# One core, four images: the low part of the normalised feature is subtracted on POOL instead of on the DVE

## The chip, the core and the metric

The kernel runs on one core of a Trainium2 chip. The metric is the device time in microseconds of one execution. The core's engines run side by side and meet at semaphores: TensorE (PE) multiplies, the DVE, ACT and POOL do elementwise work, and SP issues the DMAs.

## The reference

For each of four images (256 channels, 32 x 32 pixels) a block with a linear attention is followed by a block with a softmax attention over all 1024 pixels:

```
qkv  = x @ [wq, wk, wv]                       # 768 channels
dw   = depthwise 5x5 convolution of qkv       # 768 x 25 taps
pw   = grouped 1x1 convolution of dw
f    = concat(qkv, pw); relu(query), relu(key), value with a row of ones
out  = (value . key^T) . query, divided by its last row
x1   = batchnorm(proj . out) + x
norm = (x1 - mean(x1)) / sqrt(var(x1) + eps)   # over the pixels of a channel
F, G = f_w . norm + f_b, g_w . norm + g_b
A    = softmax(F^T . G)
y    = o_w . ((h_w . x1 + h_b) . A^T) + o_b + x1
```

## The kernel before

Each image is one `body(b)`; the first three run in a hardware loop, the last one stands behind it, without the work for a following image (`with_next` is false). While body b does the attention of image b, the engines also do most of the 5 x 5 convolution of image b + 1, in pieces that number tables place between the steps: DVE taps (`taps(n)`, L937), ACT products (`products(n)`, L748), and POOL adds (`conv_adds`, L1160), which add the ACT products to `conv`. ACT may be at most three products ahead of POOL, since `prod` has three buffers. POOL has 54 such adds for each body in the loop, numbered from 0, and none of the next image's in the last body.

Every engine runs its instructions in the order in which they are written. There is no scheduler; the order around the change is set by hand, for POOL with `RSTD_AT = (19, 20)`: after 19 and after 20 adds it takes the two small power instructions `rstd` (L1154) that give 1/sqrt(var + eps) of channel halves c = 0 and 1.

Around the change a body goes as follows. The DVE gets `x1`, its statistics (L1035 to L1041), and, after each `rstd`, `normalise(c)` (L1045), which writes the normalised half c into `nf` (a view of `rows`). ACT rounds it to the matmul type, `hi` (L848). The DVE subtracts: `lo = nf - hi` (L1066), two instructions of 128 x 1024, one for each half. PE computes F and G in eight units of 512 columns (`split_product`, the loop over `D_FG`): in each four matmuls that need only `hi` (L447, L448) and two that need `lo` (L451). Only in the first unit PE waits for `norm_lo`, between the fourth and the fifth matmul, and it wants both halves. ACT then writes `f_hi` or `g_hi` of the unit (L852), and the DVE `f_lo` or `g_lo` (L1072), which frees one of two PSUM banks for the unit after the next. The DVE has no tap between L1066 and the second `f_lo`, as its table is `TAPS_FG = (0, 0, 1, 1, 2, 1, 1, 1)`. The softmax attention (`energy`, L544, and so on) follows when all eight units are done.

There is a second subtraction of the same size, `split_lo` (L347), for the low part of the next image's input; in the loop it runs on POOL at a body's start, in the first image on the DVE.

Of the kernel before, what the change touches and what calls it, by code (L numbers as in the profile page):

```python
# [25 lines left out]
ALU = mybir.AluOpType  # L26
ACT = mybir.ActivationFunctionType
AX = mybir.AxisListType
F32 = mybir.dt.float32
# [3 lines left out]
B = 4  # L33
# [3 lines left out]
CK = C // P  # L37
# [76 lines left out]
POOL_ADDS = len(ADD_SEQ)  # L114
# [25 lines left out]
ROWS_ACT = (0, 0, 0, 0, 1, 0, 0, 0)  # L140

RSTD_AT = (19, 20)

FIRST_TAPS = 62

# [19 lines left out]
def conv_seq_kernel(nc, x, wqkv, dw, pw, proj, bn, fgw, hw, ow, l1b, masks, out):  # L165
    with ExitStack() as ctx:
        def sb(name, shape, dt=F32):
            return ctx.enter_context(nc.sbuf_tensor(name, shape, dt))

        def sem(name):  # L170
            return ctx.enter_context(nc.semaphore(name))


        hi = sb("hi", [P, CK, N], F32R)
        lo = sb("lo", [P, CK, N], F32R)
# [35 lines left out]
        nf = x_in = qp  # L211
# [51 lines left out]
        norm_ready = sem("norm_ready")  # L263
        norm_hi = sem("norm_hi")
        norm_lo = sem("norm_lo")
# [35 lines left out]
        def product_count(b, n):  # L301
            return len(FIRST_POOL_SEQ) + (PRODUCTS + LATE) * b - PRODUCTS + n

        def add_count(b, n):
            return len(FIRST_ADD_SEQ) + (POOL_ADDS + LATE - 1) * b - POOL_ADDS + n

        def late_product_count(b, n):
            return product_count(b, PRODUCTS) + n

        def late_add_count(b, n):  # L310
            return add_count(b, POOL_ADDS) + n
# [30 lines left out]
        def split_lo(engine, b):  # L342

            for h in range(2):
                engine.wait_ge(hi_ready, 2 * b + h + 1)
                cols = slice(h * HALF, (h + 1) * HALF)
                engine.tensor_tensor(lo[:, :, cols], x_in[:, :, cols], hi[:, :, cols].bitcast(F32),  # L347
                                     ALU.subtract).then_inc(lo_ready, 1)
# [23 lines left out]
        def inner(image, i):  # L372

            dy, dx = shift(i)
            return image[:, max(0, -dy):SIDE - max(0, dy), max(0, -dx):SIDE - max(0, dx)]

        def square(image):
            return image.rearrange("p (y x) -> p y x", x=SIDE)
# [12 lines left out]
        @block.sync  # L391
        def _(sp):
            def load_x(b):
                sp.dma_start(x_in[:], x[b]).then_inc(x_loaded, 16)

            def load_residual(b):
                sp.dma_start(x1[:], x[b]).then_inc(res_loaded, 16)

            def body(b, with_next, with_second):
                for q in range(2):  # L400
                    cols = slice(q * HALF, (q + 1) * HALF)
                    sp.wait_ge(pv_free, pv_count(b, 2 * (q + 1)))
                    sp.dma_start(out[b][:, :, cols], x1[:, :, cols]).then_inc(stored, 16)
                    if q == 0 and with_second:

                        sp.wait_ge(t_full, 16 * (b + 1))
                        load_x(b + 2)

                sp.wait_ge(stored, 32 * (b + 1))
                if with_next:  # L410
                    load_residual(b + 1)

            sp.dma_start(wqkv_st, wqkv).then_inc(qkv_loaded, 16)
            load_x(0)
            sp.dma_start(mask_sb[:], masks).then_inc(conv_loaded, 16)
            sp.dma_start(dw_sb[:], dw).then_inc(conv_loaded, 16)
            sp.dma_start(bn_sb[:], bn).then_inc(conv_loaded, 16)
            sp.dma_start(l1b_sb[:], l1b).then_inc(w_loaded, 16)
            sp.dma_start(fg_st, fgw).then_inc(w_loaded, 16)
            sp.dma_start(hw_st, hw).then_inc(w_loaded, 16)  # L420
            sp.dma_start(ow_st, ow).then_inc(w_loaded, 16)
            sp.dma_start(pw_sb[:], pw).then_inc(w_loaded, 16)
            sp.dma_start(proj_sb[:], proj).then_inc(w_loaded, 16)

            sp.wait_ge(d_full, D_FIRST)
            load_x(1)

            sp.wait_ge(a_free, A_FIRST)
            load_residual(0)
            with sp.Fori(0, B - 2) as b:  # L430
                body(b, True, True)
            body(B - 2, True, False)
            body(B - 1, False, False)
# [494 lines left out]
        def _(dve):  # L928
# [74 lines left out]
            def body(b, with_next):  # L1003
# [39 lines left out]
                def normalise(c):  # L1043
                    dve.wait_ge(rstd_ready, CK * b + c + 1)
                    dve.tensor_scalar(nf[:, c, :], x1[:, c, :], mv[:, c, 0:1], stat_rstd[:, c:c + 1],  # L1045
                                      ALU.subtract, ALU.mult).then_inc(norm_ready, 1)

                for u in range(D_PROJ):
                    c, h = u // 2, u % 2
# [10 lines left out]
                normalise(0)  # L1060
                taps(TAPS_NORM[1])
                normalise(1)
                for c in range(CK):
                    dve.wait_ge(norm_hi, CK * b + c + 1)
                    dve.wait_ge(norm_ready, CK * b + c + 1)
                    dve.tensor_tensor(lo[:, c, :], nf[:, c, :], hi[:, c, :].bitcast(F32),  # L1066
                                      ALU.subtract).then_inc(norm_lo, 1)
                for u in range(D_FG):
                    w, c, h = u // 4, (u // 2) % 2, u % 2
                    cols = slice(h * HALF, (h + 1) * HALF)  # L1070
# [74 lines left out]
            with dve.Fori(0, B - 1) as b:  # L1145
                body(b, True)
            body(B - 1, False)


        @block.gpsimd  # L1150
        def _(pool):
            def rstd(b, c):
                pool.wait_ge(var_ready, CK * b + c + 1)
                pool.tensor_tensor(stat_rstd[:, c:c + 1], stat_ve[:, c:c + 1], minus_half[:, c:c + 1],  # L1154
                                   ALU.pow).then_inc(rstd_ready, 1)

            def add(total, m, i):

                total, product = inner(square(total), i), inner(square(prod[:, m % PROD_BUFS, :]), i)
                pool.tensor_tensor(total, total, product, ALU.add).then_inc(conv_pool, 1)  # L1160

            def conv_adds(b, first, last):

                batch_0 = isinstance(b, int) and b == 0
                seq, adds = (FIRST_POOL_SEQ, FIRST_ADD_SEQ) if batch_0 else (POOL_SEQ, ADD_SEQ)
                for m in range(first, min(last, len(adds))):
                    t, i = adds[m]
                    n = seq.index((t, i)) + 1
                    pool.wait_ge(prod_ready, n if batch_0 else product_count(b, n))

                    if (t, i - 1) in adds:
                        before = adds.index((t, i - 1)) + 1
                        pool.wait_ge(conv_pool, before if batch_0 else add_count(b, before))
                    add(conv[:, t, :], m, i)

            def late_adds(b):

                for m in range(LATE - 1):
                    pool.wait_ge(prod_ready, late_product_count(b, m + 2))
                    if m > 0:  # L1180
                        pool.wait_ge(conv_pool, late_add_count(b, m))
                    add(late, m, LATE_SEQ[m + 1][1])

            pool.memset(raw[:], 0.0).then_inc(images_cleared, 1)

            pool.wait_ge(constants_set, 1)
            pool.wait_ge(bn_ve_ready, 1)
            pool.tensor_tensor(bn_tmp, bn_ve, minus_half, ALU.pow).then_inc(bn_rstd_ready, 1)
            conv_adds(0, 0, POOL_ADDS)
            with pool.Fori(0, B - 1) as b:  # L1190
                split_lo(pool, b + 1)
                late_adds(b)
                conv_adds(b + 1, 0, RSTD_AT[0])
                rstd(b, 0)
                conv_adds(b + 1, RSTD_AT[0], RSTD_AT[1])
                rstd(b, 1)
                conv_adds(b + 1, RSTD_AT[1], POOL_ADDS)
            late_adds(B - 1)
            rstd(B - 1, 0)
            rstd(B - 1, 1)  # L1200


def _partitioned(a, rows):
# [48 lines left out]
```

## Time and profile before

| what | value |
|---|---|
| median of 3 runs | 824.53 us (824.3 to 825.83) |
| span of the profiled execution | 823.0 us |
| PE busy | 687.7 us, 84% |
| DVE busy | 655.2 us, 80% |
| POOL busy | 544.9 us, 66% |
| ACT busy | 477.8 us, 58% |
| mean granted TensorE clock | 0.944 of full |

The span runs from the first to the last instruction of the profiled execution. That execution has no time of its own among the three runs; the median of these is 1.53 us above its span, which is what lies around the span. Busy shares are means over stages with different limits, so the stage around the subtraction is read by itself below. A granted clock of 1.00 is TensorE's 2.4 GHz, 0.50 its 1.2 GHz.

### The profile page before, as it was taken

The numbers are of one execution on the slowest core, as the hardware profiler recorded it, in microseconds if no ns is written. First come the engines' busy times: TensorE is split into PE (matmuls) and PEld (weight loads), VectorE is DVE, ScalarE is ACT, GpSimd is POOL, SyncE is SP. The second block draws the span as 40 slices with busy tenths as digits, with TensorE's granted clock in tenths as the row PEclk, the third lists the DMA queues.
The fourth block names the chain that finished last, engine by engine and source line by source line (L and its number), as shares of the span: only waits on it lengthen the run. The fifth ranks groups of instructions, "written<-read, shape, count | busy, mean of one in ns | idle before, by whom it ended". The sixth has DMA issues, their size and how long they took to land.

```text
span 823.0 us, 9427 instructions
## 1 busy us (share of the span) xinstructions
PE 687.7 (84%) x2892; PEld 466.7 (57%) x2892; DVE 655.2 (80%) x797; ACT 477.8 (58%) x703; POOL 544.9 (66%) x248
## 2 busy tenths in 40 slices
PE   4999888779678899789677899789677994788997
PEld 4744577566456467576456457475456454455843
DVE  6999599899779889989779889989779899334520
ACT  4944458674568668673568668773567646213520
POOL 3498958896779798895769889785769858100000
PEclk9999999899799999889799999889799998999999
DMA  5000020000000130000000021000000001000000
GB/s 196 2 0 1 0 103 1 2 0 1 0 2 1 38 115 2 0 0 0 0 0 0 26 84 44 0 0 0 0 0 0 26 26 51 1 0 1 1 25 25
DMA packets 4801, 15.93 MB, mean 19 GB/s; under 512 B 672, under 2 KB 928, under 8 KB 3744
## 3 DMA queue, kind: packets, MB, share of 16 engines
q1 hardware_dynamic: 4768, 15.56, 5.1%
q8 instruction: 12, 0.20, 0.1%
q14 instruction: 21, 0.17, 0.1%
HBM read 11.37 MB, written 4.19 MB: 19 GB/s over the span
## 4 chain that ended last, share of the span: by engine, by line
PE 49%; DVE 32%; issue 12%; ACT 4%; DMA 1%; DVEq 0%; ACTq 0%; SPq 0%
DVE ps L937 17%; PE ps L568 13%; PE ps L544 7%; PE ps L494 7%; PE ps L517 3%; PE ps L622 3%; PE ps L451 3%; PE ps L447 3%; PE ps L448 3%; DVE sd L981 2%; PE ps L559 2%; DVE kv L999 2%; DVE den L997 2%; DVE small L1090 2%; PE ps L504 1%
## 5 line engine op out<-in xcount | busy, mean ns | idle before, releaser
L1160 POOL TENSOR_TENSOR conv<-conv,prod 128x930 f32<-128x930 f32 (+4 forms) x192 | 435.8, 2301 | 101.4 <-ACT prod L748 97.9
L937 DVE SCALAR_TENSOR_TENSOR ps<-raw,dw_sb,ps 128x960 f32<-128x960 f32 (+4 forms) x290 | 348.5, 1202 | 12.8 <-issue 4.8
L748 ACT ACTIVATE prod<-raw,dw_sb 128x930 f32<-128x930 f32 (+4 forms) x228 | 248.7, 1115 | 74.9 <-POOL conv L1160 62.1
L568 PE MATMUL ps<-kv,oc 128*128 128x512 f32 x256 | 111.6, 594 | 2.8 <-ACT kv L878 2.8
L1160 POOL TENSOR_TENSOR rows<-rows,prod 128x930 f32<-128x930 f32 (+4 forms) x36 | 83.2, 2312 | 15.0 <-ACT prod L748 12.3
L517 PE MATMUL ps<-sd,rows 128*128 128x144 f32 x256 | 56.0, 372 | 32.5 <-DVE kv L999 19.3
L568 PEld LDWEIGHTS ps<-kv,oc 128*128 128x128 f32 x256 | 48.3, 190 | 61.4 <-issue 57.4
L517 PEld LDWEIGHTS ps<-sd,rows 128*128 128x128 f32 x256 | 45.8, 246 | 45.3 <-DVE kv L999 28.0
L1090 DVE TENSOR_REDUCE small<-ps 128x1 f32<-128x1024 f32 x32 | 39.1, 1221 | 28.9 <-PE ps L544 28.9
L862 ACT ACTIVATE rows<-ps,small 128x1024 f32<-128x1024 f32 x32 | 35.7, 1116 | 45.3 <-DVE small L1090 45.3
L622 PE MATMUL ps<-oc,proj_sb 128*128 128x512 f32 x128 | 56.0, 595 | 2.1 <-DVE kv L999 1.3
L559 PE MATMUL ps<-mask_sb,rows 128*128 128x128 f32 x256 | 36.5, 282 | 24.7 <-ACT kv L878 14.7
L878 ACT COPY kv<-ps 128x512 f32<-128x512 f32 x64 | 34.6, 587 | 26.5 <-PE ps L559 26.5
L544 PE MATMUL ps<-g_hi,f_hi 128*128 128x512 f32 x128 | 43.1, 419 | 7.5 <-DVE g_lo L1072 7.5
L559 PEld LDWEIGHTS ps<-mask_sb,rows 128*128 128x128 f32 x256 | 27.4, 140 | 38.3 <-ACT kv L878 24.1
L447 PE MATMUL ps<-hi,wqkv_hi 128*128 128x512 f32 x96 | 39.4, 410 | 10.3 <-DVE lo L347 10.3
L774 ACT COPY oc<-ps 128x512 f32<-128x512 f32 x32 | 16.4, 599 | 53.1 <-PE ps L528 53.1
L447 PE MATMUL ps<-hi,fg_hi 128*128 128x512 f32 x64 | 31.8, 496 | 17.9 <-ACT hi L848 11.8
L766 ACT ACTIVATE kv<-ps 128x256 f32<-128x256 f32 x68 | 30.5, 449 | 23.9 <-PE ps L583 21.5
L1154 POOL TENSOR_TENSOR small<-small 128x1 f32<-128x1 f32 x8 | 4.9, 612 | 59.3 <-DVE small L1041 59.3
L622 PEld LDWEIGHTS ps<-oc,proj_sb 128*128 128x128 f32 x128 | 24.0, 190 | 31.7 <-issue 28.7
L544 PE MATMUL ps<-g_lo,f_hi 128*128 128x512 f32 x128 | 41.1, 403 | 0.0
(97 smaller groups left out, 1172.3 us busy)
## 6 DMA issues: line engine op xcount, KB each, us to landing
rows<-x_dram SPq DMA_DIRECT2D x4, 1024.0 KB, 4.8
x<-x_dram SPq DMA_DIRECT2D x4, 1024.0 KB, 4.9
out_dram<-x SPq DMA_DIRECT2D x8, 512.0 KB, 3.1
conv<-wqkv_dram SPq DMA_DIRECT2D x1, 768.0 KB, 4.6
conv<-fg_dram SPq DMA_DIRECT2D x1, 512.0 KB, 5.4
proj_sb<-proj_dram SPq DMA_DIRECT2D x1, 512.0 KB, 7.3
pw_sb<-pw_dram SPq DMA_DIRECT2D x1, 384.0 KB, 6.5
conv<-hw_dram SPq DMA_DIRECT2D x1, 256.0 KB, 5.6
```

The costliest lines, as they stand in the source:

```text
L447: pe.matmul(dst, lh, rh, start=(k == 0), stop=False)
L494: mm = pe.matmul(dst, diagonal(t, i), view, start=(i == 0), stop=(i == taps - 1))
L517: mm = pe.matmul(dst[:, h * SDW:(h + 1) * SDW], qp[:, h, j * P:(j + 1) * P], sd[:, h, :], start=True, stop=True)
L544: mm = pe.matmul(ps[:, pair + h, :], lhs, g[:, k, h * HALF:(h + 1) * HALF], start=(s == 0), stop=(s == len(steps) - 1))
L559: mm = pe.transpose(ps[:, 4 + u, j * P:(j + 1) * P], rows[:, i % ROW_BUFS, key:key + P], ident)
L568: mm = pe.matmul(ps[:, 4 + c, :], ht[:, j, c * P:(c + 1) * P], pt[:, j, :], start=(j == 0), stop=(j == NB - 1))
L622: mm = pe.matmul(d_bank(s), proj_sb[:, k, c * P:(c + 1) * P], oc[:, k, h * HALF:(h + 1) * HALF], start=(k == 0), stop=(k == 2 * CK - 1))
L748: act.activation(dst, view, ACT.Copy, scale=weight(t, i)).then_inc(prod_ready, 1)
L862: act.activation(rows[:, i % ROW_BUFS, :], ps[:, pair:pair + 2, :].rearrange("p a n -> p (a n)"), ACT.Exp, bias=neg_max[:, i:i + 1], accum ...
L937: return dve.scalar_tensor_tensor(dst, view, w, before, ALU.mult, ALU.add)
L1090: dve.tensor_reduce(neg_max[:, i:i + 1], ps[:, pair:pair + 2, :].rearrange("p a n -> p (a n)"), AX.X, ALU.max, negate=True).then_inc(max_r ...
L1160: pool.tensor_tensor(total, total, product, ALU.add).then_inc(conv_pool, 1)
```

## The change

The DVE no longer issues the two subtractions of a body. POOL issues them: in a loop body after add 22 and ahead of add 23 of the next image's convolution, in the last body right behind the second `rstd`. The operands, the waits (`norm_ready`, `norm_hi`) and the semaphore that is raised (`norm_lo`) are the same.

```diff
 RSTD_AT = (19, 20)
+NORM_LO_AT = 23
...
                 taps(TAPS_NORM[1])
                 normalise(1)
-                for c in range(CK):
-                    dve.wait_ge(norm_hi, CK * b + c + 1)
-                    dve.wait_ge(norm_ready, CK * b + c + 1)
-                    dve.tensor_tensor(lo[:, c, :], nf[:, c, :], hi[:, c, :].bitcast(F32),
-                                      ALU.subtract).then_inc(norm_lo, 1)
...
+            def norm_split(b):
+                for c in range(CK):
+                    pool.wait_ge(norm_ready, CK * b + c + 1)
+                    pool.wait_ge(norm_hi, CK * b + c + 1)
+                    pool.tensor_tensor(lo[:, c, :], nf[:, c, :], hi[:, c, :].bitcast(F32),
+                                       ALU.subtract).then_inc(norm_lo, 1)
...
                 rstd(b, 1)
-                conv_adds(b + 1, RSTD_AT[1], POOL_ADDS)
+                conv_adds(b + 1, RSTD_AT[1], NORM_LO_AT)
+                norm_split(b)
+                conv_adds(b + 1, NORM_LO_AT, POOL_ADDS)
             late_adds(B - 1)
             rstd(B - 1, 0)
             rstd(B - 1, 1)
+            norm_split(B - 1)
```

POOL's queue in the loop body, before, from the second `rstd` on (`small` is the result of `rstd`; the adds write `conv`):

```order
L1154 TENSOR_TENSOR small<-small 128x1 [waits var_ready]
L1169 REGISTER_ALU
L1173 REGISTER_ALU [waits prod_ready]
L1160 TENSOR_TENSOR conv<-conv,prod 128x32x30 [waits conv_pool]
L1169 REGISTER_ALU
L1173 REGISTER_ALU [waits prod_ready]
L1160 TENSOR_TENSOR conv<-conv,prod 128x32x30 [waits conv_pool]
L1173 REGISTER_ALU [waits prod_ready]
```

The same place of the changed kernel, from the second of these adds (21) to add 23:

```order
L1163 TENSOR_TENSOR conv<-conv,prod 128x32x30 [waits conv_pool]
L1176 REGISTER_ALU [waits prod_ready]
L1163 TENSOR_TENSOR conv<-conv,prod 128x32x31 [waits conv_pool]
L1157 TENSOR_TENSOR lo<-rows,hi 128x1024 [waits norm_hi,norm_ready] x2
L1172 REGISTER_ALU
L1176 REGISTER_ALU [waits prod_ready]
L1163 TENSOR_TENSOR conv<-conv,prod 128x32x31 [waits conv_pool]
```

The two subtractions stand between adds 22 and 23, which follow one another before; in the changed file the adds have line 1163 and the subtractions line 1157.

The DVE's queue in the loop body, before, around its subtractions:

```order
L937 SCALAR_TENSOR_TENSOR ps<-raw,dw_sb,ps 128x960 [waits conv_dve]
L1044 REGISTER_ALU
L1045 TENSOR_SCALAR rows<-x,mv,small 128x1024 [waits rstd_ready]
L1066 TENSOR_TENSOR lo<-rows,hi 128x1024 [waits norm_ready,norm_hi] x2
L1071 ISA
L1072 SCALAR_TENSOR_TENSOR f_lo<-ps,l1b_sb,f_hi 128x512 [waits fg_hi_ready]
L1071 REGISTER_ALU
```

And in the changed kernel:

```order
L938 SCALAR_TENSOR_TENSOR ps<-raw,dw_sb,ps 128x960 [waits conv_dve]
L1045 REGISTER_ALU
L1046 TENSOR_SCALAR rows<-x,mv,small 128x1024 [waits rstd_ready]
L1067 ISA
L1068 SCALAR_TENSOR_TENSOR f_lo<-ps,l1b_sb,f_hi 128x512 [waits fg_hi_ready]
```

Behind the second `normalise` the DVE now has only the wait for the first `f_hi`. No tap moved into the place.

## Rows read from the trace of the kernel before

**Rows 1.** The page: the chain that ended last, shares of the span by engine.

```profile
PE 49%; DVE 32%; issue 12%; ACT 4%; DMA 1%; DVEq 0%; ACTq 0%; SPq 0%
```

**Rows 2.** The longest waits of PE: us in total, times, longest.

```profile
PE ps L451 <- DVE lo L1066: 10.8, 4, 3.7
```

**Rows 3.** Timeline of body 1, DVE: start, us, instructions, idle before.

```profile
390.44 1.17 DVE L1045 TENSOR_SCALAR rows<-x,mv,small 128x1024 f32<-128x1024 f32 x1
...
392.66 1.60 DVE L1045 TENSOR_SCALAR rows<-x,mv,small 128x1024 f32<-128x1024 f32 x1
394.19 6.57 DVE L1066 TENSOR_TENSOR lo<-rows,hi 128x1024 fp32r<-128x1024 f32 x2
402.80 0.75 DVE L1072 SCALAR_TENSOR_TENSOR f_lo<-ps,l1b_sb,f_hi 128x512 fp32r<-128x512 f32 x1 [2.04 <-ACT f_hi L852]
```

**Rows 4.** Timeline of body 1, POOL, in narrow windows: adds 20 to 24 singly.

```profile
388.80 2.27 POOL L1160 TENSOR_TENSOR conv<-conv,prod 128x960 f32<-128x960 f32 x1
...
391.02 2.70 POOL L1160 TENSOR_TENSOR conv<-conv,prod 128x960 f32<-128x960 f32 x1
...
393.68 2.76 POOL L1160 TENSOR_TENSOR conv<-conv,prod 128x992 f32<-128x992 f32 x1
...
396.40 3.27 POOL L1160 TENSOR_TENSOR conv<-conv,prod 128x992 f32<-128x992 f32 x1
...
403.94 2.28 POOL L1160 TENSOR_TENSOR conv<-conv,prod 128x960 f32<-128x960 f32 x1 [4.27 <-ACT prod L748]
```

**Rows 5.** Timeline of body 1, ACT and PE around the wait.

```profile
394.30 1.06 ACT L848 ACTIVATE hi<-rows 128x1024 fp32r<-128x1024 f32 x1 [0.16 <-DVE rows L1045]
...
400.81 1.22 PE L451 MATMUL ps<-lo,fg_hi 128*128 128x512 f32 x2 [3.59 <-DVE lo L1066]
...
402.07 0.69 ACT L852 ACTIVATE f_hi<-ps,l1b_sb 128x512 fp32r<-128x512 f32 x1 [6.71 <-PE ps L451]
402.66 1.13 ACT L748 ACTIVATE prod<-raw,dw_sb 128x960 f32<-128x960 f32 x1
404.63 0.69 ACT L852 ACTIVATE f_hi<-ps,l1b_sb 128x512 fp32r<-128x512 f32 x1 [0.85 <-PE ps L451]
```

**Rows 6.** Body 0: add 22 on POOL, the DVE's pair.

```profile
206.32 2.75 POOL L1160 TENSOR_TENSOR conv<-conv,prod 128x992 f32<-128x992 f32 x1
...
206.82 6.56 DVE L1066 TENSOR_TENSOR lo<-rows,hi 128x1024 fp32r<-128x1024 f32 x2
```

**Rows 7.** The other subtraction of this size, by source line and timeline.

```profile
L347 POOL TENSOR_TENSOR lo<-rows,hi x6: 2361/2366/2382, 114.7 to 488.0; 128x1024 fp32r<-128x1024 f32 x6
L347 DVE TENSOR_TENSOR lo<-rows,hi x2: 1219/1222/1226, 9.0 to 10.1; 128x1024 fp32r<-128x1024 f32 x2
...
298.20 4.69 POOL L347 TENSOR_TENSOR lo<-rows,hi 128x1024 fp32r<-128x1024 f32 x2
```

**Rows 8.** Timeline of the last body: DVE, ACT, PE.

```profile
735.11 0.81 DVE L1045 TENSOR_SCALAR rows<-x,mv,small 128x1024 f32<-128x1024 f32 x1 [0.44 <-POOL small L1154]
741.04 2.36 DVE L1066 TENSOR_TENSOR lo<-rows,hi 128x1024 fp32r<-128x1024 f32 x2 [5.11 <-ACT hi L848]
...
743.45 0.73 PE L451 MATMUL ps<-lo,fg_hi 128*128 128x512 f32 x2 [0.25 <-DVE lo L1066]
...
748.56 0.69 ACT L852 ACTIVATE f_hi<-ps,l1b_sb 128x512 fp32r<-128x512 f32 x1 [1.09 <-PE ps L451]
...
751.80 0.69 ACT L852 ACTIVATE g_hi<-ps,l1b_sb 128x512 fp32r<-128x512 f32 x1 [1.10 <-PE ps L451]
```

**Rows 9.** Windows: stretch, length, busy (x) of PE, PEld, DVE, ACT, POOL, PEclk.

```profile
396.00:406.20 10.20, 6.61 (x16) 4.63 (x16) 6.26 (x4) 3.28 (x4) 5.93 (x3) 0.50 0.00 0
...
744.05:747.45 3.40, 3.40 (x10) 2.62 (x9) 0.75 (x1) 1.36 (x2) 0.00 (x0) 0.50 0.00 0
747.50:757.00 9.50, 8.68 (x35) 5.75 (x33) 4.50 (x6) 3.98 (x6) 0.00 (x0) 1.00 0.00 0
```

## The prediction

> **What bounds the kernel now.** I read the chain that ended last first: PE and DVE hold it together (49% and 32%), ACT has 4%, and POOL does not appear [rows 1]. So POOL's 66% busy share is beside the path, and work given to POOL is free as long as nobody on the path waits for it. The waits of PE then show whether the subtraction is on the path: PE waits for `lo` four times, once in each body, 10.8 us together [rows 2]. It is work that PE waits for directly, not cover work. The question is therefore not how much DVE time is freed, but when the second half of `lo` is there.
>
> In body 1 the DVE takes up the pair at 394.19 and ends it at 400.76, 3.3 us for each instruction [rows 3], where the same operation on a DVE beside an idle POOL takes 1.22 [rows 7], and 1.2 in the last body, where POOL has no adds either (2.36 for both) [rows 8]. The rows of POOL say what is in between [rows 4]. Add 22 ends at 396.44, and the first subtraction, 1.2 us long, then ends near 397.5. Add 23, begun at 396.40 by its record, lasts 3.27 in place of some 2.2 and ends at 399.67; the second subtraction ends 1.1 us later. The two engines take turns: a subtraction is held until the running add ends, and the next add is held until the subtraction ends. The pair is thus a sum of waits: add 22's rest (2.2 us), 1.2, add 23 (2.2), 1.2.
>
> The rule for this is in the Trainium skill, "SBUF — State Buffer", section "Who interferes with whom": DVE and GpSimd share one port pair as an exclusive lock, for a whole instruction. The trace agrees (3.3 us against 1.22). It alone would speak for the change, since a pair on one engine has no such turn to wait for.
>
> **The change, part by part.**
>
> *The DVE loses two instructions a body.* That frees 6.57 us of each of three bodies and 2.36 us of the last. All of it becomes waiting: the next thing in the DVE's order is the first `f_lo`, which waits for ACT's `f_hi`, which waits for PE, which waits for `lo`; no tap stands between (the order in the section on the change). Gain from the DVE's time: 0. What hides that nothing is gained is a wait of 2.04 us [rows 3] that becomes about 8.9 (2.04 + 6.57 and the delay below).
>
> *POOL's price.* It runs the same subtraction in 2.37 us, and two in a row in 4.69 [rows 7]. The shape there is 2 x 512 columns, here 1024 in one piece; adds of 960 columns take 2.27 and 2.28 when undisturbed [rows 4], which for 1024 would be 2.4. Bounds for the pair: below 4.5 (twice the undisturbed 960-column add, less a little for overlap), above 5.5 (twice the 2.76 of a disturbed add). I take 4.69, the row of the same operation, since the DVE is idle meanwhile.
>
> *When POOL begins, three loop bodies.* POOL takes the pair behind add 22. Adds 20 and 21 and the two `normalise` run as before, so add 22 ends at 396.44 again. By then both halves of `hi` are ready (the second ends at 394.30 + 1.06 = 395.36 [rows 5]), so nothing else is waited for. Add 22 begins next to the end of `normalise` (394.26), and 394.26 + 2.2 gives 396.4: its stretch comes from there, not from the subtraction behind it. The pair ends at 396.40 + 4.69 = 401.09, against 400.76: +0.33 us. Body 0: 206.32 + 2.75 = 209.07, less the same 0.04 of overlap, plus 4.69 is 213.72, against 206.82 + 6.56 = 213.38: +0.34 [rows 6]. Body 2 repeats body 1. Three bodies: +1.0 us (bounds +0.4 with 4.5, +3.4 with 5.5).
>
> *Add 23 and what is queued behind it.* It now begins at 401.1 instead of 396.4 and, no longer held, ends at about 403.4 instead of 399.67. Nobody waits for it in that time: POOL stood idle for 4.27 us until the product of add 24 came [rows 4]. That product begins at 402.66 and takes 1.13 [rows 5]; it comes 0.33 later, so add 24 begins near 404.3 with 0.9 us to spare. Cost: 0. If the cover were gone, each microsecond that POOL is late would push the products that come before `g_hi` in ACT's order, and through them PE, one for one.
>
> *The last body.* Here POOL is idle, so there is no turn to save. The DVE begins at 741.04 and ends the pair at 743.40, and PE resumes at 743.45 [rows 8]. POOL can begin at 741.05, when the first half of `hi` is there, and ends at 741.05 + 4.69 = 745.74. PE: +2.34 us (bounds +2.1 and +3.1).
>
> On that ratio the Trainium skill, "GPSIMD Engine Reference", section "Elementwise — side-by-side cycle accounting", gives 4497 against 2293 ns for an add of 2048 float32 columns; half of it, an estimate, is 2.25 us for one subtraction, and by it the sum below would be about 1 us smaller. The rows show 2.37 against 1.22, and I go by them.
>
> *TensorE's clock.* In body 1 the granted clock is 0.50, the 1.2 GHz level, from 396.0 to 406.2 [rows 9]: it falls after PE had stood idle for the first `hi`, and stays low through the idle 3.59 us before L451; it rises 5.4 us after PE resumes at 400.81. While it is low a unit takes 404.63 - 402.07 = 2.56 us [rows 5]; at 2.4 GHz two take 751.80 - 748.56 = 3.24, so 1.62 each [rows 8]. A microsecond of work at the low level thus costs 0.37. In the loop bodies PE's idle time hardly changes (3.59 to 3.9 us), and I leave the clock as it is. In the last body PE was idle for only 0.25 us before L451, and the clock was low for 3.4 us, 744.05 to 747.45. After the change it is idle there for about 2.6 us, more like a loop body. If the clock rises when it does now, 1.65 us of low work remain and 0.65 us comes back; if it rises 5.4 us after PE resumes, 2.0 us more low work costs +0.74. I take +0.4, nearer to the second, since the idle time is nearer to that of the loop bodies.
>
> **Sum.** 1.0 + 2.34 + 0.4 = +3.7 us. On the profiled execution's span that is 823.0 + 3.7 = 826.7; the median stands 1.53 above that span, so the time is 828.2 us, 0.45% more than before. With the bounds: +0.4 + 2.1 - 0.65 = +1.9, and +3.4 + 3.1 + 0.74 = +7.2 (831.7), which needs every instruction disturbed by an engine that is idle. A change within 0.2% (1.65 us) is about what a measurement of this kernel cannot tell from none.
>
> **The rivals.**
>
> *Shorter adds.* If the DVE's held subtraction also slows the add that runs, add 22 falls from 2.76 to 2.2 and the pair ends 0.55 - 0.33 = 0.2 us earlier than before. For: both records are long. Against: `normalise` explains it to a tenth. Three times -0.2, and 2.34 with nothing for the clock, is +1.7: 826.2. Chance 0.07.
>
> *Faster, by the clock.* The low level in a loop body costs 5.4 x 0.37 = 2.0 us. If another rhythm around the wait (POOL's pair ends 0.3 us later, the engines' loads differ) let the clock rise as soon as PE resumes, three bodies would give back 6.0, and the sum is 1.0 + 2.34 - 6.0 = -2.7: 821.8. For: in the last body the low stretch is only 3.4 us. Against: the clock falls at 396.0, before anything differs. It decides when less than about 2.5 us of low work remain in each loop body. Chance 0.04.
>
> *POOL becomes late.* If the pair takes 5.5 or more, or adds run longer than the 0.9 us to spare, add 24 slips and ACT's products with it: +3.4 from the pair and 2.34 + 0.4, some +6: 830.7. For: POOL's records stretch to 3.27. Against: they do so only beside a DVE that works. Chance 0.07.
>
> *It doesn't matter.* Later waits in the loop bodies (PE for the attention's rows) swallow the 1.0 us, and the last body's clock returns 0.65 and some of what is queued behind is hidden: +1.2, 825.7. Against: the chain runs through PE, `f_lo` and `energy` without a gap. Chance 0.06.
>
> The forecast has the rest, 0.76. Its own range is 826.4 to 829.9. The time is named for it alone; the range 826.0 to 830.2 leaves out the clock rival, most of the last one and about half of the late POOL, with a small part of the forecast, under 2 in 10. Faster by over 0.2%: 0.04. Within 0.2%: the last rival, part of the first, and a thin edge of the forecast, 0.11. Slower: 0.85.
>
> **What the profile of the changed kernel would show.** Right: in body 1 two POOL subtractions of 2.35 each directly behind add 22, the DVE idle for about 8.9 us before its first `f_lo`, PE's wait for `lo` at 3.9 us in loop bodies and 2.6 in the last (some 14 us in all, from 10.8), add 23 of 2.3 us and a short idle time before add 24. Wrong: subtractions over 2.6 us, POOL idle before them (then `hi` is late, not the adds), an add 22 of 2.2 us, or ACT waiting for POOL before `g_hi`. A low stretch of the clock in the last body much over 3.4 us puts me at the upper end; low stretches under 8 us in loop bodies put me at the lower.

## The result and the profile after

| | before | changed |
|---|---|---|
| median | 824.3 us (822.79 to 828.62, 15 runs) | 829.55 us (827.88 to 831.78, 15 runs) |
| span of the profiled execution | 823.0 us | 827.4 us |
| mean granted clock | 0.944 | 0.94 |

The ratio is 1.006, with a 95% interval of 1.0046 to 1.0075. By the medians the changed kernel is 5.2 us slower where 3.7 were forecast, and its median lies inside the stated range of 826.0 to 830.2 us, near the upper end.

First the waits of PE, which answer to [rows 2]: us in total, times, longest.

```profile
PE ps L452 <- POOL lo L1157: 13.9, 4, 3.9
```

PE waits for `lo` as often as before, now for POOL, and 3.1 us longer in all (10.8 before).

The timeline of body 1 follows, first POOL and then the DVE, ACT and PE. This execution stood 1.39 us later than the one of before already when the body's first `rstd` began (385.86 against 384.47), so times are compared from that instruction on.

```profile
385.86 0.55 POOL L1150 TENSOR_TENSOR small<-small 128x1 f32<-128x1 f32 x1 [8.74 <-DVE small L1042]
...
390.19 7.63 POOL L1163 TENSOR_TENSOR conv<-conv,prod 128x960 f32<-128x960 f32 x3
397.78 4.65 POOL L1157 TENSOR_TENSOR lo<-rows,hi 128x1024 fp32r<-128x1024 f32 x2
402.39 2.31 POOL L1163 TENSOR_TENSOR conv<-conv,prod 128x992 f32<-128x992 f32 x1
405.60 2.27 POOL L1163 TENSOR_TENSOR conv<-conv,prod 128x960 f32<-128x960 f32 x1 [0.90 <-ACT prod L749]
...
404.46 0.75 DVE L1068 SCALAR_TENSOR_TENSOR f_lo<-ps,l1b_sb,f_hi 128x512 fp32r<-128x512 f32 x1 [8.81 <-ACT f_hi L853]
...
403.74 0.69 ACT L853 ACTIVATE f_hi<-ps,l1b_sb 128x512 fp32r<-128x512 f32 x1 [7.00 <-PE ps L452]
...
408.29 0.69 ACT L853 ACTIVATE f_hi<-ps,l1b_sb 128x512 fp32r<-128x512 f32 x1 [0.30 <-PE ps L452]
...
402.49 1.22 PE L452 MATMUL ps<-lo,fg_hi 128*128 128x512 f32 x2 [3.80 <-POOL lo L1157]
```

The pair stands right behind adds 20 to 22 and takes 4.65 us. It ends at 402.43, that is 16.57 after the `rstd` (402.43 - 385.86); the DVE's pair of before ended at 400.76, 16.29 after it [rows 3]. Add 23 is back at 2.31 us, from 3.27 [rows 4], and POOL still idles for 0.90 before add 24. The DVE waits 8.81 us for the first `f_hi`. The first `f_hi` begins 17.88 after the `rstd` (17.60 before), the third 22.43. The third of before, and the last `g_hi` of its last body, for the comparison further down:

```profile
406.79 0.69 ACT L852 ACTIVATE f_hi<-ps,l1b_sb 128x512 fp32r<-128x512 f32 x1 [0.45 <-PE ps L451]
...
756.47 0.69 ACT L852 ACTIVATE g_hi<-ps,l1b_sb 128x512 fp32r<-128x512 f32 x1 [0.75 <-PE ps L451]
```

The last body, again POOL, ACT and PE:

```profile
731.91 0.55 POOL L1150 TENSOR_TENSOR small<-small 128x1 f32<-128x1 f32 x1 [28.38 <-DVE small L1042]
...
742.59 4.65 POOL L1157 TENSOR_TENSOR lo<-rows,hi 128x1024 fp32r<-128x1024 f32 x2 [6.07 <-ACT hi L849]
...
760.95 0.69 ACT L853 ACTIVATE g_hi<-ps,l1b_sb 128x512 fp32r<-128x512 f32 x1 [0.72 <-PE ps L452]
...
747.30 1.22 PE L452 MATMUL ps<-lo,fg_hi 128*128 128x512 f32 x2 [2.65 <-POOL lo L1157]
```

And windows of both places: stretch, length, busy time (and instructions) of PE, PEld, DVE, ACT and POOL, and the granted clock.

```profile
397.20:407.40 10.20, 6.40 (x16) 4.50 (x15) 1.13 (x2) 2.80 (x4) 9.30 (x5) 0.50 0.00 0
...
745.40:752.20 6.80, 4.90 (x12) 3.84 (x13) 1.11 (x2) 1.37 (x2) 1.84 (x1) 0.50 0.00 0
```

In the loop body the stretch at the half clock is as long as before, 10.2 us [rows 9]. In the last body it is 6.8 us, from 3.4.

Where did the 4.4 us between the two spans come from? The first `rstd` of the first body and that of the last body, before and then after:

```profile
197.11 0.55 POOL L1154 TENSOR_TENSOR small<-small 128x1 f32<-128x1 f32 x1 [7.00 <-DVE small L1041]
...
730.47 0.55 POOL L1154 TENSOR_TENSOR small<-small 128x1 f32<-128x1 f32 x1 [28.49 <-DVE small L1041]
```

```profile
198.36 0.55 POOL L1150 TENSOR_TENSOR small<-small 128x1 f32<-128x1 f32 x1 [7.01 <-DVE small L1042]
...
731.91 0.55 POOL L1150 TENSOR_TENSOR small<-small 128x1 f32<-128x1 f32 x1 [28.38 <-DVE small L1042]
```

1.25 us lie ahead of the first of them, where nothing was changed. The clock can account for them: ahead of that `rstd` it is low for 10.2 us in the profile of before and for 13.7 in the one after, and 3.4 us more at the prediction's 0.37 are 1.26. The three loop bodies add (731.91 - 198.36) - (730.47 - 197.11) = 0.19 us, and what follows the last one adds (827.4 - 731.91) - (823.0 - 730.47) = 2.96 us.

### The profile page after: what moved, and what is told of

Same layout as the page of the kernel before. It is cut to its first block, busy times and chain, and to the rows that moved or that the text cites. A ratio compares the mean times of both kernels' runs of the same rounds, so it can differ in the third digit from the quotient of the medians.

```text
span 827.4 us, 9427 instructions
## 1 busy us (share of the span) xinstructions
PE 689.5 (83%) x2892; PEld 468.4 (57%) x2892; DVE 634.0 (77%) x789; ACT 477.4 (58%) x703; POOL 560.1 (68%) x256
## 4 chain that ended last, share of the span: by engine, by line
PE 50%; DVE 29%; issue 11%; ACT 5%; POOL 2%; DMA 1%; POOLq 0%; DVEq 0%; ACTq 0%; SPq 0%
DVE ps L938 16%; PE ps L569 13%; PE ps L545 7%; PE ps L495 7%; PE ps L518 4%; PE ps L452 3%; PE ps L448 3%; PE ps L623 3%; PE ps L449 3%; DVE sd L982 2%; PE ps L560 2%; PE ps L505 2%; POOL lo L1157 2%; DVE kv L1000 2%; DVE small L1086 2%
## 5 line engine op out<-in xcount | busy, mean ns | idle before, releaser
L1068 DVE SCALAR_TENSOR_TENSOR f_lo<-ps,l1b_sb,f_hi 128x512 fp32r<-128x512 f32 x16 | 12.0, 750 | 51.1 <-ACT f_hi L853 51.1
```

## The experiments

Each time below is a median and stands against the median of the kernel before on the same chip. The difference in us that follows a ratio is worked out from the ratio; that of the two medians can be some 2 us away from it. "Low" is a stretch at the half clock, and a "last stretch" runs from the first `rstd` of the last body to the end.

**The change in one part of the program at a time.** The first kernel leaves the last body's pair on the DVE:

```diff
                 normalise(1)
+                for c in range(CK) if not with_next else ():
+                    dve.wait_ge(norm_hi, CK * b + c + 1)
+                    dve.wait_ge(norm_ready, CK * b + c + 1)
+                    dve.tensor_tensor(lo[:, c, :], nf[:, c, :], hi[:, c, :].bitcast(F32),
+                                      ALU.subtract).then_inc(norm_lo, 1)
...
-            norm_split(B - 1)
```

> POOL subtracts in the three loop bodies, the DVE in the last one. Theory (what counts is when the second half of lo is there): POOL's pair ends 0.3 us later than the DVE's in each loop body, and part of that is given back by the clock, so +0.2 to +1.0 us against the kernel before, and PE's wait for lo in the loop bodies near 3.9 us, in the last 0.25. Rival (the loop bodies carry what the medians show beyond my sum, +5.25 measured against about 3 in the last body): +2.3 us or more.

The second leaves the loop bodies' pair on the DVE (`if with_next`, and `norm_split(b)` taken out of the loop).

> The DVE subtracts in the loop bodies, POOL in the last. Theory: nearly all of the loss is here, 2.34 us from the slower pair and some 0.4 to 0.7 from the clock, +2.5 to +3.1 us against the kernel before. Rival (the loss is spread over the four bodies): +1.3 us, a quarter of +5.25.

Measured: the loop alone 827.09 against 825.1 us, ratio 1.0016 (1.0002 to 1.0031), +1.3 us. The last body alone 828.68 against 825.1, ratio 1.0041 (1.0024 to 1.0057), +3.4 us. Together 4.7, most of it in the last body, as the theory has it. +3.4 is a little above the 2.5 to 3.1 expected, which its interval holds. An even split is out, by the last stretches of the profiles above all. In the profile of the first, PE waits 11.1 us for POOL three times and 0.3 for the DVE; its last stretch takes 826.1 - 733.49 = 92.6 us, as before (92.5), the second 827.3 - 731.68 = 95.6, as the changed kernel (95.5). +1.3 is above my 0.2 to 1.0; whether it is different from nothing the control at the end puts in doubt.

**One add earlier, one add later.**

```diff
-NORM_LO_AT = 23
+NORM_LO_AT = 22
```

> As the changed kernel, with the pair one add earlier, behind add 21. Theory: POOL begins when the first half of hi is there (394.2 in the times of the kernel before) and ends at 398.8 instead of 401.1, 2.3 us earlier in each loop body, and with the last body's loss of 3 the sum is -1.9 x 3 + 3 = -2.7 us against the kernel before. Rival (another thing than the pair sets the end of the stage, such as POOL being late for add 24 and ACT's products behind it): within 1 us of the changed kernel, so about +4 to +5.

> As the changed kernel, with the pair one add later, behind add 23. Theory: one add of 2.3 us more ahead of PE's wait in each loop body, +6.9 us against the changed kernel, about +11 to +12 against the kernel before, and PE waits 6.2 us for lo in a loop body. Rival (the wait has slack behind it): under +3 us against the changed kernel.

Measured: one earlier 820.37 against 825.1, ratio 0.9936 (0.9914 to 0.9958), -5.3 us; one later 838.08 against 825.1, ratio 1.0132 (1.0099 to 1.0165), +10.9 us. The direction is the theory's in both. The later place costs about what was expected (+11 to +12; the medians are 13.0 apart). The earlier place gives twice what was expected, and more than the shift of the pair itself explains: the pair ends 2.1 us earlier in each loop body, and from the first body's `rstd` to the last body's it takes 523.0 us (723.05 - 200.03) against 533.55, 3.5 us less for each. Its timeline in body 1, POOL and PE:

```profile
387.93 4.91 POOL L1163 TENSOR_TENSOR conv<-conv,prod 128x960 f32<-128x960 f32 x2
393.41 4.66 POOL L1157 TENSOR_TENSOR lo<-rows,hi 128x1024 fp32r<-128x1024 f32 x2 [0.57 <-DVE rows L1046]
398.02 4.60 POOL L1163 TENSOR_TENSOR conv<-conv,prod 128x992 f32<-128x992 f32 x2
...
398.12 1.22 PE L452 MATMUL ps<-lo,fg_hi 128*128 128x512 f32 x2 [1.97 <-POOL lo L1157]
```

And the window of its low stretch:

```profile
395.20:402.10 6.90, 4.93 (x12) 3.37 (x11) 0.75 (x1) 1.87 (x3) 6.90 (x4) 0.51 0.00 0
```

PE's wait in body 1 falls from 3.80 to 1.97 us, and the low stretch falls from 10.2 to 6.9. In the later place it is 13.7 us long, with a wait of 5.8 to 6.1. Its windows, of body 1 and of the last body:

```profile
400.90:414.50 13.60, 6.92 (x15) 4.96 (x16) 1.06 (x2) 3.51 (x5) 10.42 (x5) 0.50 0.00 0
752.50:762.60 10.10, 8.21 (x18) 5.95 (x19) 1.50 (x2) 1.43 (x3) 3.91 (x2) 0.50 0.00 0
```

In the loop bodies the low stretch moves with PE's wait; in the expectation for the earlier place I had left it as it was. In the last body it doesn't: nothing differs there from the changed kernel, PE waits for 1.79 us, less than the 2.65 of that kernel, and the low stretch is 10.2 us in place of 6.8. It begins earlier there, so the four matmuls ahead of the wait are slow too, and that shortens the wait.

The same place without the last body's loss (pair behind add 21 in the loop, the DVE's pair in the last body):

> POOL subtracts behind add 21 in the loop bodies, the DVE in the last. Theory: the loop's gain of the run with the pair behind add 21, without the last body's loss of about 3 us: -8 to -9 us against the kernel before (that run was at -5.3). Rival (the last body's loss depends on where the clock stands, not on the pair): -5 to -6.

Measured: 816.43 against 823.85, ratio 0.9911 (0.9886 to 0.9935), -7.3 us. It lies between the -8 to -9 of the theory and the -5 to -6 of the rival, and 2 us below the run with POOL in the last body, with intervals that overlap, so the times don't decide between the two. The profile does: it gives the last stretch as 92.6 us (813.2 - 720.58) against 95.5 (818.6 - 723.05). The last body's 3 us are there again.

**The engines' turns.** The kernel before, with POOL held out of the pair's way:

```diff
                 rstd(b, 1)
-                conv_adds(b + 1, RSTD_AT[1], POOL_ADDS)
+                conv_adds(b + 1, RSTD_AT[1], 22)
+                pool.wait_ge(norm_lo, CK * b + CK)
+                conv_adds(b + 1, 22, POOL_ADDS)
```

> The kernel before, with one wait added on POOL: in a loop body it takes add 22 only when both of the DVE's subtractions are done. Theory (the DVE's pair is long only because it takes turns with POOL's adds): each subtraction takes 1.2 us, the pair ends at 396.6 instead of 400.76 in each loop body, -4.1 us three times, and the clock stays low for a shorter stretch: -12 to -16 us against the kernel before, PE's wait for lo near 0.2 in all four bodies. Rival (POOL, held for 3 us and with adds 22 and 23 still to do, becomes late for ACT's products and gives the gain back later in the stage): under -6 us. Rival (a DVE subtraction is slow beside other engines' traffic anyway): it stays at 3.3 us and the time rises.

Measured: 810.5 against 823.85 us, ratio 0.9827 (0.9812 to 0.9841), -14.3 us, inside the expected -12 to -16. It is the fastest kernel of this study, faster than every version of the change. The DVE's subtractions in its profile by source line (min/median/max in ns, first and last start):

```profile
L1066 DVE TENSOR_TENSOR lo<-rows,hi x8: 1210/1221/1226, 209.0 to 731.2; 128x1024 fp32r<-128x1024 f32 x8
```

Its timeline in body 1: the pair, POOL behind it, and PE.

```profile
391.07 2.43 DVE L1066 TENSOR_TENSOR lo<-rows,hi 128x1024 fp32r<-128x1024 f32 x2
...
393.66 20.12 POOL L1160 TENSOR_TENSOR conv<-conv,prod 128x992 f32<-128x992 f32 x9 [3.06 <-DVE lo L1066]
...
394.24 1.05 PE L451 MATMUL ps<-lo,fg_hi 128*128 128x512 f32 x2
```

All eight subtractions take 1.2 us, where the six of the loop bodies took 3.3, with nothing changed but POOL's absence: that POOL's adds stretch the pair is shown. That the two engines take whole turns, and don't merely slow each other, is read from the rows of before, whose ends such turns give to a tenth; no run separates the two. PE goes from the fourth matmul to the fifth without a wait. The low stretch of body 1 is still 6.8 us long:

```profile
391.50:398.20 6.70, 5.83 (x14) 4.58 (x15) 2.75 (x3) 2.76 (x4) 4.54 (x2) 0.50 0.00 0
```

POOL idles for 3.06 us and then works through nine adds without a gap; that backlog costs little here. The Trainium skill, "SBUF — State Buffer", section "Who interferes with whom", calls the port pair that the DVE and GpSimd share an exclusive lock, which a DVE instruction with two SBUF inputs and a GpSimd instruction that reads SBUF contend for. The trace agrees: 1.2 us alone, 3.3 beside the adds.

With the hold one add earlier (21 in place of 22):

> As the run that holds POOL ahead of add 22, with the hold one add earlier. Theory: the second normalise, 1.6 us beside POOL's add, falls to 0.8, but the second half of hi comes only 0.2 us earlier, since ACT is busy with the first half; POOL loses another 2.2 us. Within 1.5 us of that run if POOL has room, 3 us or more above it if it hasn't (adds 21 to 23 then end after the product of add 24 is there).

Measured: 818.53 against 823.85 us, ratio 0.9949 (0.9932 to 0.9967), -4.2 us, 10 us above the hold ahead of add 22 by the ratios and 8 by the medians. The two profiled spans are only 3.3 us apart (815.6 and 812.3), since the profiled execution of the one is the fastest of its six (817.44) and that of the other the slowest of its five (814.1). The profiles thus show only a part of the loss. The size stays open, the sign is clear. POOL has no room for one add more. PE's waits for `g_lo` before a unit show it, first of this kernel and then of the one that holds ahead of add 22:

```profile
PE ps L447 <- DVE g_lo L1072: 9.8, 3, 3.3
```

```profile
PE ps L447 <- DVE g_lo L1072: 5.5, 3, 2.2
```

In the kernel before they are 4.9 us. PE's waits for `f_lo` grow too, to 4.7 us in nine, from 0.2 in the hold ahead of add 22.

ACT makes three products ahead of the sixth unit's `g_hi`, and each needs a buffer that POOL must have freed; the `g_lo` behind that `g_hi` frees the bank of the eighth unit.

**The clock.** The changed kernel with work for PE in its wait, results never read:

```diff
+                def before_lo(b):
+                    for n in range(8):
+                        pe.matmul(a_bank(n), fg_hi[:, 0, 0, 0:P], hi[:, 0, 0:HALF], start=True, stop=True)
+                    pe.wait_ge(norm_lo, CK * (b + 1))
```

`before_lo(b)` stands in place of the wait for `norm_lo`.

> The changed kernel, with eight matmuls more of 512 columns between PE's fourth matmul and its wait for lo, in each body; their results are never read. They take 1.8 us at the full clock and 3.4 at the half, less than the wait of 3.9, so the wait ends when it did. Theory (part of the loss is the clock, which stays low for longer when PE idles): the low stretch falls from 10.2 to about 6.8 us in a loop body and from 6.8 to 3.4 or less in the last, at 0.37 us for each, so -4 to -5 us against the changed kernel, near the kernel before or below it. Rival (only the wait counts, the clock follows another thing): within 1 us of the changed kernel, or above it in the last body.

Measured: 817.95 against 823.85 us, ratio 0.9928 (0.9915 to 0.9941). Against the changed kernel's ratio of 1.006 that is -10.9 us, by matmuls whose results nobody uses. The timeline of body 1, POOL's pair and PE:

```profile
395.11 4.70 POOL L1162 TENSOR_TENSOR lo<-rows,hi 128x1024 fp32r<-128x1024 f32 x2
...
395.86 2.94 PE L642 MATMUL ps<-hi,fg_hi 128*128 128x512 f32 x8
399.86 0.73 PE L452 MATMUL ps<-lo,fg_hi 128*128 128x512 f32 x2 [1.05 <-POOL lo L1162]
```

And windows of body 1 and of the last body:

```profile
394.40:397.90 3.50, 3.50 (x9) 2.72 (x9) 0.00 (x0) 0.00 (x0) 3.50 (x3) 0.51 0.00 0
398.00:408.00 10.00, 8.69 (x34) 5.63 (x33) 4.92 (x6) 6.40 (x9) 9.62 (x5) 1.00 0.00 0
730.00:760.00 30.00, 24.41 (x102) 17.79 (x101) 9.38 (x13) 10.65 (x16) 4.71 (x2) 1.00 0.00 1
```

POOL's pair is as long as ever, and PE resumes 16.67 us after the body's first `rstd` (399.86 - 383.19), as in the changed kernel (402.49 - 385.86 = 16.63). So nothing of the gain comes from an earlier end of the wait. But the low stretch is 3.5 us in place of 10.2, and the last body has none around the wait. Over the whole execution, the mean granted clock is 0.959 against 0.94 in the changed kernel, which makes 67 us of low time (2 x 0.041 x 816.2) against 99 (2 x 0.06 x 827.4). At the 0.37 us that the prediction put on a microsecond of low work, 32 us are at most 12; the ratios give 10.9 and the spans 11.2. The expectation was too small, since I had counted only 3.4 us less for each loop body. The stretch around the wait lost 6.8 there, and a second one of 3.4 us later in the body (from 421.1 on in the changed kernel) is gone as well: from 400 to 440 the clock is at its full level.

The same in the last body only:

> The changed kernel with the eight extra matmuls between PE's fourth matmul and its wait for lo in the last body only; their results are never read. PE is idle 2.65 us there and the low stretch is 6.8 us, against 3.4 in the kernel before. Theory (the last body's loss of 3.0 is 2.3 of the slower pair and the rest of the clock): the low stretch goes, and with it 5 us of work at the half clock, -1.2 to -2.0 us against the changed kernel, +3 to +4 against the kernel before. Rival (the last body's loss is all waiting): no difference to the changed kernel, +5 against the kernel before.

Measured: 828.14 against 825.14 us, ratio 1.0035 (1.0021 to 1.0048), 2.1 us below the changed kernel by the ratios, with intervals that just touch. The profile has no low stretch around the last body's wait. PE resumes there 15.44 us after the `rstd` (748.28 - 732.84), as late as in the changed kernel (15.39), and the last stretch is 93.8 us (826.6 - 732.84) against 95.5: 1.7 us less, inside the expected 1.2 to 2.0, and all of it the clock's.

Filling was then tried on the fastest kernel, in the other idle time of the stage, ahead of PE's wait for `hi`:

```diff
+                for n in range(10):
+                    pe.matmul(d_bank(do["fg"]), fg_hi[:, 0, 0, 0:P],
+                              fg_hi[:, 1, :, :].rearrange("p k m -> p (k m)"), start=True, stop=True)
                 pe.wait_ge(norm_hi, CK * (b + 1))
```

> The run that holds POOL ahead of add 22 (-14.3 us), with ten matmuls more of 512 columns before PE's wait for hi in each body; they read weights only and their result is overwritten. At the full clock they take 2.3 us of an idle time of 3.1 (2.6 in the last body). Theory (the low stretch of 6.8 us in each loop body and 3.4 in the last comes from PE standing idle before hi): it falls to 3.4 or to nothing, and 0.37 of each microsecond comes back, so -3 to -9 us against that run, -17 to -23 against the kernel before. Rival (that idle time is too short to matter, the clock falls for something earlier): within 1.5 us of that run.

Measured: 814.05 against 825.14 us, ratio 0.9854 (0.9832 to 0.9877), -12.0 us. The -17 to -23 that I expected did not come: there is no gain on the -14.3 of the kernel without it, and whether the 2 us less are real the overlapping intervals leave open. Its windows of body 1:

```profile
392.00:409.00 17.00, 13.82 (x52) 8.87 (x51) 12.28 (x13) 12.44 (x16) 13.93 (x7) 1.00 0.00 0
409.20:419.40 10.20, 7.61 (x17) 5.55 (x18) 5.55 (x6) 3.50 (x5) 7.31 (x4) 0.50 0.00 0
```

And PE in its timeline, at the last of the eight units:

```profile
410.22 0.80 PE L447 MATMUL ps<-hi,fg_hi 128*128 128x512 f32 x1 [3.27 <-DVE g_lo L1075]
```

The clock now stays at its full level through the first units, so the expected part came. But the units arrive sooner at the place where ACT waits for POOL's backlog; PE stands idle there for 3.27 us, and a low stretch of 10.2 us follows. The idle time and the low clock moved, they didn't go. The rival's "that idle time is too short to matter" was wrong, and so was my gain.

**The control.**

> The kernel before, unchanged, against itself: what the comparison and the profile give when nothing is different. The ratio should hold 1 in its interval. In the profiles so far the first small power instruction of POOL in body 0, ahead of which no kernel was changed, stands anywhere from 197.1 to 200.1 us. Theory (that is the scatter of one execution): here it stands later than the 197.1 of the first profile, by chance somewhere in that range. Rival (the changed kernels have a slower start, since their program is laid out otherwise): it stands at 197.1 again.

> The changed kernel, unchanged, a second time on one chip with the control. By its profile the change costs 0.2 us in the three loop bodies together and 3.0 in the last, 3.2 in all, while the 15 runs say +5.25. Theory (what is beyond 3.2 is scatter in where the clock is low): the ratio is 1.004 to 1.006, and the loop bodies cost under 1 us together again. Rival (the loop bodies cost 1 us or more each in most executions, and the profile caught one where they did not): more than 2 us in the three loop bodies of this profile.

Measured: the kernel before against itself 825.34 and 824.1 us, ratio 1.0022 with an interval of 1.0004 to 1.0039, which does not hold 1. The changed kernel again 829.78 against 824.1, ratio 1.0077 (1.0064 to 1.009), above the 1.004 to 1.006 that I expected. So two equal kernels can come out 0.2% apart, and differences up to about that are not shown by ratios: neither the +1.3 us of the loop alone, nor the 2 us between pairs of runs above. The first `rstd` stands at 198.13 in this profile of the kernel before and at 198.68 in the changed one; over all the profiles it lies between 197.1 and 200.1. The slow start is not tied to the change; the 197.1 of the first profile is the low end of a scatter of 3 us. The low time ahead of that `rstd` scatters too: 10.2 us in the first profile, 13.7 in the control. From the first `rstd` to the last, the control takes 532.61 us (730.74 - 198.13) and the changed kernel 533.65 (732.33 - 198.68). With the first pair of profiles (533.36 and 533.55) the loop bodies cost 0.2 and 1.0 us, all three together: small, and not 1 us each, so the rival of more than 2 us is out. The last stretch is 92.1 against 95.6 us, +3.5.

## Why the prediction was right, point by point

**What bounds.** PE's wait for the second half of `lo` decides. Shown from both sides: with the pair one add later +10.9 us, one earlier -5.3, without turns -14.3.

**The DVE's freed time is worth nothing.** Its wait for the first `f_hi` grew to 8.81 us (8.9 forecast), and no other of its instructions moved into the freed place.

**POOL's price.** 4.65 us for the pair against 4.69; by the Trainium skill, "GPSIMD Engine Reference", section "Elementwise — side-by-side cycle accounting", the estimate from its 4497 ns for 2048 columns was 2.25 for one, and 2.34 is measured (median of eight). Here the measurement decides, 4% above.

**Three loop bodies, +1.0 us.** The pair ended 0.28 us later by the timeline (0.33 forecast). That it reached the end undiminished is the part that did not hold in the first pair of profiles: by the third `f_hi` the delay is 0.11 (22.43 against 406.79 - 384.47 = 22.32, from the timeline of before), since the low stretch ended at the same distance from the start of the body, so that a later start met less of it. Together the loop bodies cost 0.2 us in one pair of profiles and 1.0 in the other, so the term was too high in the first and met in the second.

**Add 23.** It ended with 0.90 us to spare, as forecast. The runs with a hold one add earlier and with more matmuls show what it costs when that room is gone: PE waits up to 3.3 us for a bank that `g_lo` has to free.

**The last body, +2.34 us and +0.4 for the clock.** PE's L452 begins 15.39 us after the first `rstd` (747.30 - 731.91), L451 before 12.98 (743.45 - 730.47): +2.41. At the last `g_hi` the delay is 3.04 us (760.95 - 731.91 = 29.04, before 756.47 - 730.47 = 26.00). The rest, 0.63, is the clock: the low stretch doubled from 3.4 to 6.8 us. The clock's term of 0.4 was a third too small, with its sign and its reason right. The run that fills PE's wait in this body only took the low stretch away, and with it 1.7 us at an unchanged end of the wait.

**The sum.** +3.7 forecast; the two pairs of profiles average +4.75 (827.65 against 822.9), of which 0.9 lies ahead of the first `rstd` and is scatter as far as can be seen. The remaining 3.85 answers to the sum of 3.7. It does so partly by luck: in the first pair the loop bodies cost 0.2 where their term had 1.0, and the last body 2.96 where its terms had 2.74, 3.15 in all. The medians give +5.2, and +5.7 in the repetition. The 1.5 us by which +5.2 exceeds the forecast is in no term of the sum, and with a control that is 1.2 us from itself, I can't say whether it is real.

**The rivals.** "Faster, by the clock" was put at 0.04 and did not happen by itself. Its mechanism is real, though, and larger than its price of 2.0 us a body: filling PE's wait gave 10.9 us, by the profiles 3.4 in each loop body (from the first body's `rstd` to the last body's 722.39 - 198.96 = 523.43, against 533.55). "POOL becomes late" happened in two experiments, not in the change. "Shorter adds" is out: adds 20 to 22 take 7.63 us, as they did (396.44 - 388.80 = 7.64, [rows 4]), with no subtraction of the DVE's queued behind add 22. Of "It doesn't matter" one half came in the first pair of profiles, where the loop bodies' delay was nearly swallowed; the last body's was not.

What the prediction did not see is that the wait was worth more than its length. It priced the low clock only where it changed in the last body, and took it as given in the loop. The range was wide enough for that. But when I then asked what the stage could give, I expected 1.9 us a body from the earlier place, by the same reasoning, where it gave 3.5.

## What to carry to other kernels

An instruction that is slow because two engines take turns is not mended by merely handing it to the slower of the two, in the same place: that cost 0.6% here. One add earlier the same move gave 0.6%, but better still was to leave it where it was. Keep it on the faster engine and keep the other one out of its way for that moment, if that one has room: one wait gave 1.7% here. And price a wait of TensorE with the clock behind it, not only by its length.

## What the runs showed of the hardware

In the loop bodies of the kernel before and of those where POOL subtracts, the low stretches of the granted clock around the wait for `lo` were longer where PE waited longer: with a wait of up to 6.1 us it was 13.7, with 3.9 it was 10.2, with 1.97 it was 6.9. In the last body, where PE's idle time for `hi` is shorter (2.58 us against 3.07), 2.65 us went with 6.8 and 0.25 with 3.4. The wait alone doesn't set the length, though: with 1.79 us it was 10.2 in the last body of the kernel with the later place, and with no wait at all it was 6.8 in bodies 1 and 2 of the kernel with the hold ahead of add 22, and 3.4 in body 0. What else sets it stays open. I had not expected that eight matmuls with no use in each body take 10.9 us off a kernel, nor that taking away one idle time only moved the low stretch to the next.
